# Feed-forward stage: row scaling moved to ScalarE, two small operations per scale, twelve steps written out in a new order

## The chip, the cores and the metric

One NeuronCore of a Trainium2 chip runs the whole program. The metric is the device time of one execution in microseconds. The core has TensorE (PE), VectorE (DVE), ScalarE (ACT), GpSimd (POOL) and a sync queue (SP) that here only starts transfers. Each engine runs its own queue in order, and waits on semaphores that instructions of other engines raise.

## The reference

The reference applies four attention layers and four feed-forward layers to x (8 batches, 256 rows, 256 columns). Only the last feed-forward is touched; x is normalised over its columns first, and the hidden width is 1024:

```python
def act_quant(x):
    scale = 127.0 / jnp.clip(jnp.max(jnp.abs(x), axis=-1, keepdims=True), 1e-05)
    return jnp.clip(jnp.round(x * scale), -128, 127) / scale
...
h = bit_linear(x, w1)
h = depthwise_conv1d(h.transpose(0, 2, 1), conv_w, conv_b)
h = h.transpose(0, 2, 1)
h = jax.nn.silu(h)
return bit_linear(h, w2)
```

`bit_linear` multiplies rows rounded by `act_quant` with weights rounded to -1, 0 and 1. The convolution has three taps along the 256 rows of a batch. The result is added to x. Each row is thus scaled and rounded twice: once before the first product (256 columns), once before the second (1024 columns).

## The kernel before, in words

`build` runs one stage after another. The last is `bit_ffn` (from line 2520); it begins at 1536 us of the span and lasts to the end. A batch has TB = 2 tiles of 128 rows, and the hidden columns are FT = 8 groups of 128 (index f). What happens to a batch, by engine and line:

- VectorE: `norm` (L2615) writes xn for each tile. `token_scale` finds the largest absolute value of each row (amax, L2622) and from it, in four small operations, the factor qs = 127 / max (L2630) and its inverse qr (L2632).
- ScalarE: `rounded` (L2727) writes q1 = xn * qs + MAGIC for each tile; adding MAGIC rounds to a whole number. VectorE: `unrounded` (L2641) writes q2 = (q1 - MAGIC) * qr for each tile.
- TensorE: `turn_tokens` (L2805) transposes q2 into PSUM. ScalarE's `high_part` (L2734) and VectorE's `low_part` (L2646) take it out as xh and xl.
- TensorE: `hidden` (L2817) multiplies for each f, with four matmuls, into one of three PSUM banks. ScalarE's `middle_tap` (L2741), then VectorE's `first_tap` (L2651) and `last_tap` (L2656) apply the convolution. A bank is free when its last tap is done: hidden f waits for the last tap of f - 3, and hidden 0, 1 and 2 for the last taps of f = 6, 7 and 5 of the batch before (lines 2813 to 2815).
- ScalarE: `silu` (L2749) in two halves of four f each. The first silu is preceded by a load of the function table.
- TensorE: `turn_silu` (L2828) transposes one tile at a time into the one PSUM tile pn, 128x1024. The next tile can come in when s1 of the tile before is written (line 2826).
- VectorE: `tile_scale` in six parts: the largest absolute value of each row of pn (L2665), four small operations (L2670 to L2678, which give sqs and sqr), and s1 = pn * sqs + MAGIC (L2683), 128x1024. GpSimd: `whole` (L2787) writes sq = s1 - MAGIC in bf16.
- TensorE: `turn_back` (L2837) transposes sq; ScalarE's `turned_back` (L2756) takes it out as sqT; `product` (L2846) multiplies with the second weights. VectorE's `residual` (L2690) scales by sqr and adds to x. SP stores a batch when both its residuals are done (L2581).

The work is staged in twelve steps, n = 0 to 11. In step n batch n is `new` (norm, token_scale, rounded), batch n - 1 is `turn` (unrounded, turned, split), batch n - 2 is `hid` (hidden and taps), batch n - 3 is `end` (turn_silu, tile_scale, whole) and batch n - 4 is `last` (products, residuals). Steps 4 to 7 have all five and are called full. The order inside a step is written out by hand on each engine: VectorE's loop runs over places (place 2f is the first tap of f, place 2f + 1 the last tap), ScalarE's and TensorE's over f. `every_step` (L2560) writes ten steps as code: 0 to 3, then 4 and 5 in a hardware loop of two turns, which are steps 4 to 7, then 8 to 11. Waits are counted by `upto` (L2573), in the loop from a register.

## Time and profile before

| | |
|---|---|
| Time, three runs | 1704.36, 1704.78 (median), 1707.48 us |
| The profiled execution's own time | 1701.18 us |
| Its span, first to last instruction | 1699.3 us |
| Granted TensorE clock, mean | 0.937 of full |
| Busy over the whole span | TensorE 86%, VectorE 57%, ScalarE 38%, GpSimd 25% |
| The feed-forward stage | 1536.2 to 1699.3 us |

The profiled execution is one run and lies 3.6 us below the median of the timed ones. In its trace an instruction has a start, counted from the beginning of the span, a duration, an engine, a line, and the tiles written and read. The duration of a pipelined instruction is longer than the time until the next one can start.

### The profile page before, as it was taken

Reading aid. Unit: us, or ns where it says so; the run is one execution under the profiler, and the core shown is the slowest. Engines: PE = TensorE matmul, PEld = TensorE weight load, DVE = VectorE, ACT = ScalarE, POOL = GpSimd, SP = SyncE. Lnnn points to the kernel's source line nnn. Section 1 sums busy time; section 2 is a strip of 40 time slices with the busy share of each in tenths; the row PEclk is TensorE's granted clock in tenths of the full one; section 3 lists DMA queues with packets and bytes.
Section 4 is the critical chain, followed back from the end, with each engine's and each line's share of the span. In section 5 each row is a group of like instructions: output and inputs, shape, how many; then the busy total and the mean of one; then the engine's idle time right before and its main releaser. Section 6 shows DMA issues by size and latency. Waiting matters only on the chain. (4 is left out here: it accounts for less than half of the span.)

```text
span 1699.3 us, 32774 instructions
## 1 busy us (share of the span) xinstructions
PE 1460.4 (86%) x11594; PEld 1279.2 (75%) x11594; DVE 971.9 (57%) x2432; ACT 638.2 (38%) x1413; POOL 423.8 (25%) x655
## 2 busy tenths in 40 slices
PE   4789997499977999999997699999999988875765
PEld 3456664489966788888886599999999976654654
DVE  4666763312224676666665655555555547767896
ACT  1233332112214444445443244444444423234553
POOL 2011101133304444434332111100000036730212
PEclk8899999699998999999999799999999999996788
DMA  7655330684410000010000444045337221100000
GB/s 149 114 94 108 67 50 14 236 279 148 133 41 25 8 8 20 20 29 20 8 1 19 159 171 168 30 175 176 132 110 277 87 75 48 34 7 1 14 12 26
DMA packets 97294, 139.83 MB, mean 82 GB/s; under 512 B 10080, under 2 KB 81248, under 8 KB 97056
## 3 DMA queue, kind: packets, MB, share of 16 engines
q1 hardware_dynamic: 79792, 109.83, 22.2%
q0 software_dynamic: 6368, 18.62, 3.8%
q10 hardware_dynamic: 11024, 9.97, 1.9%
q8 instruction: 63, 1.03, 0.3%
q14 instruction: 47, 0.39, 0.1%
HBM read 111.12 MB, written 14.42 MB: 74 GB/s over the span
## 5 line engine op out<-in xcount | busy, mean ns | idle before, releaser
L1867 PE MATMUL f_ph<-f_xgT,f_w 128*128 128x128 f32 x2496 | 285.3, 275 | 2.9 <-issue 2.0
L1867 PEld LDWEIGHTS f_ph<-f_xgT,f_w 128*128 128x128 f32 x2496 | 282.1, 192 | 3.6 <-issue 3.6
L1031 ACT ACTIVATE a_work<-a_ps,a_bias 128x128 f32<-128x128 f32 (+1 forms) x256 | 104.1, 419 | 172.6 <-issue 98.0
L1962 DVE TENSOR_TENSOR f_w_low<-f_w,f_w_high 128x2048 fp32r<-128x2048 f32 x39 | 89.4, 2292 | 99.9 <-ACT f_w_high L1921 99.9
L1231 POOL TENSOR_TENSOR a_work<-a_work,a_recip 128x256 f32<-128x256 f32 (+1 forms) x128 | 103.1, 827 | 147.0 <-DVE a_recip L1150 145.9
L1836 POOL DMA_INDIRECT f_xg<-normed_x,order x39 | 37.1, 952 | 345.2 <-PE f_px L1856 331.6
L574 DVE CUSTOM_DVE_ANT_0 a_shut_s<-a_ps,a_neg 128x256 f32<-128x256 f32 x256 | 93.0, 420 | 39.9 <-PE a_ps L253 39.3
L486 ACT ACTIVATE a_pT<-a_ps 128x1024 f32<-128x1024 f32 x64 | 65.5, 1024 | 119.5 <-PE a_ps L253 119.5
L1921 ACT ACTIVATE f_w_high<-f_w 128x2048 fp32r<-128x2048 f32 x39 | 74.5, 1910 | 85.6 <-DVE f_yg L1974 83.3
L1155 DVE TENSOR_TENSOR a_qk<-a_ps,a_qk 128x512 fp32r<-128x512 f32 x64 | 44.2, 691 | 96.4 <-ACT a_qk L1048 96.4
L1666 PEld LDWEIGHTS f_ph<-f_xgT,f_w 128*128 128x128 f32 x736 | 86.8, 195 | 6.2 <-DMA f_w<-in_f_w 3.0
L1878 PE MATMUL f_py<-f_w_high,f_h_high 128*128 128x256 f32 x312 | 91.4, 293 | 0.0
L1666 PE MATMUL f_ph<-f_xgT,f_w 128*128 128x128 f32 x736 | 87.7, 278 | 3.5 <-DMA f_w<-in_f_w 2.8
L1878 PE MATMUL f_py<-f_w_high,f_h_low 128*128 128x256 f32 x312 | 88.1, 282 | 0.0
L1878 PE MATMUL f_py<-f_w_low,f_h_high 128*128 128x256 f32 x312 | 88.0, 282 | 0.0
L1967 DVE TENSOR_TENSOR f_h_low<-f_raw,f_h_high 128x512 fp32r<-128x512 f32 x78 | 56.4, 723 | 54.3 <-ACT f_h_high L1925 54.3
L1925 ACT ACTIVATE f_h_high<-f_raw 128x512 fp32r<-128x512 f32 x78 | 49.2, 631 | 91.7 <-DVE f_raw L1982 91.7
L1676 PE MATMUL f_py<-f_w,f_hT 128*128 128x256 f32 x368 | 83.5, 380 | 0.2 <-ACT f_hT L1708 0.2
L1747 DVE TENSOR_SCALAR f_hT<-f_ph,f_b 128x128 f32<-128x128 f32 x92 | 25.9, 344 | 88.0 <-PE f_ph L1666 88.0
L1676 PEld LDWEIGHTS f_py<-f_w,f_hT 128*128 128x128 f32 x368 | 68.1, 190 | 9.0 <-issue 0.4
L1708 ACT ACTIVATE f_hT<-f_ph,f_b 128x128 f32<-128x128 f32 x92 | 26.2, 368 | 121.0 <-PE f_ph L1666 121.0
L1132 DVE TENSOR_REDUCE a_top_s<-a_ps 128x2 f32<-128x256 f32 (+1 forms) x128 | 64.1, 542 | 6.2 <-PE a_ps L917 6.2
(348 smaller groups left out, 3465.2 us busy)
## 6 DMA issues: line engine op xcount, KB each, us to landing
f_w<-in_f_w SPq DMA_DIRECT2D x70, 1024.0 KB, 6.8
sorted_y<-f_yg ACTq DMA_DIRECT2D x62, 128.0 KB, 1.7
a_qs<-a_part SPq DMA_DIRECT2D x48, 128.0 KB, 4.3
a_ks<-a_part SPq DMA_DIRECT2D x42, 128.0 KB, 6.2
normed_x<-a_xn SPq DMA_DIRECT2D x16, 256.0 KB, 2.2
x<-in_x SPq DMA_DIRECT2D x8, 256.0 KB, 6.7
a_mask<-in_mask SPq DMA_DIRECT2D x8, 256.0 KB, 6.4
a_maskT<-in_maskT SPq DMA_DIRECT2D x8, 256.0 KB, 6.5
```

Of the source, the lines that this page charges most:

```text
L486: act.activation(pT[:, u // 2 % 2, 2 * (u % 2):2 * (u % 2) + 2, :, :].rearrange("p j t n -> p j (t n)"), ps[:, ST:ST + 2, :], ACT.Exp, sca ...
L574: a = dve.tensor_tensor_reduce(out=shut_s[:, j, t, :], in0=ps[:, bank(m) + j, t * S:(t + 1) * S], in1=neg[:, m // U % 3, t, :], scale=1.0, ...
L1031: act.activation(prob[:, s, i, t * P:(P if t == 0 else TRI)], ps[:, SB + 2 * s + i, t * S:(t * S + P * (t + 1))], ACT.Exp, bias=bias[:, s, ...
L1132: dve.tensor_reduce(top_s[:, s, t, :], ps[:, SB + 2 * s:SB + 2 * s + 2, t * S:t * S + P * (t + 1)], AX.X, ALU.max).then_inc(max_done, 1)
L1231: pool.tensor_tensor(part, part, recip[:, s, t, :].unsqueeze(2).to_broadcast([P, 2, P * (t + 1)]), ALU.mult).then_inc(shares_done, 1)
L1666: mm = pe.matmul(ph[:, q, n, f * P:(f + 1) * P], w[:, s, k, (q * FQ + f) * P:(q * FQ + f + 1) * P], xgT[:, s, k, :], start=(k == 0), stop= ...
L1676: mm = pe.matmul(py[:, s, 0:D], hT[:, s, f, :], w2[:, s, f, :], start=(f == 0), stop=(f == FT - 1))
L1867: mm = pe.matmul(ph[:, q, n, f * P:(f + 1) * P], w[:, s, k, (q * FQ + f) * P:(q * FQ + f + 1) * P], xgT[:, s, k, :], start=(k == 0), stop= ...
L1878: mm = pe.matmul(py[:, s, 0:D], hT[a][:, s, f, :], w2_parts[b][:, s, f, :], start=(f == 0 and n == 0), stop=(f == FT - 1 and n == len(PASS ...
L1921: act.activation(w2_parts[0][:, s, :, :], w2[:, s, :, :], ACT.Copy).then_inc(w2_high, 1)
L1962: dve.tensor_tensor(w2_parts[1][:, s, :, :], w2[:, s, :, :], w2_parts[0][:, s, :, :], ALU.subtract).then_inc(w2_low, 1)
L1967: dve.tensor_tensor(hT[1][:, s, q * FQ:(q + 1) * FQ, :].rearrange("p f n -> p (f n)"), raw[:, q, :], hT[0][:, s, q * FQ:(q + 1) * FQ, :].r ...
```

## The change

The diff is cut to its core. Calls of `upto(pair, ...)` become plain numbers, `every_step` goes, and all twelve steps are written out on each engine by `for n in range(B + 4): step(n)`.

- A scale takes two small operations where it took four: unit = max(maximum, 1e-5) / 127, and its reciprocal. For rows of x, qr is that unit. For hidden rows, sqr = sunit * unit is a small product on GpSimd, in front of `whole`, with a semaphore of its own.
- s1 is written by ScalarE (`scaled`) instead of VectorE.
- The pieces of a step have other places on VectorE, ScalarE, GpSimd and TensorE. For tile 1 `turn_silu`, the reciprocal, s1 and `whole` move into the step after, with batch n - 4; so do silu half 1 (with n - 3) and `turn_back` of tile 0.
- Waits are changed to suit.

```diff
-            def token_scale(pair, b, k):
+            def token_scale(b, k):
 
                 if k == 0:
-                    dve.wait_ge(xn_done, upto(pair, 2 * b + 1, 2))
+                    dve.wait_ge(xn_done, 2 * b + 2)
                     ins = dve.tensor_reduce(amax[:, :], xn[:, :, :], AX.X, ALU.max, apply_absolute_value=True)
                 else:
-                    dve.wait_ge(prep, upto(pair, 5 * b + k - 1, 5))
+                    dve.wait_ge(prep, 3 * b + k)
                 if k == 1:
-                    ins = dve.tensor_scalar(amaxc[:, :], amax[:, :], 1e-5, None, ALU.max)
+                    ins = dve.tensor_scalar(qr[:, :], amax[:, :], 1e-5, 1.0 / 127.0, ALU.max, ALU.mult)
                 if k == 2:
-                    ins = dve.reciprocal(rec[:, :], amaxc[:, :])
-                if k == 3:
-                    ins = dve.tensor_scalar(qs[:, :], rec[:, :], 127.0, None, ALU.mult)
-                if k == 4:
-                    ins = dve.tensor_scalar(qr[:, :], amaxc[:, :], 1.0 / 127.0, None, ALU.mult)
+                    ins = dve.reciprocal(qs[:, :], qr[:, :])
                 ins.then_inc(prep, 1)
...
-                dve.wait_ge(red_done, upto(pair, 5 * i + k - 1, 5 * TB))
+                dve.wait_ge(red_done, 3 * i + k)
                 if k == 1:
-                    dve.tensor_scalar(saxc[:, c], sax[:, c], 1e-5, None, ALU.max).then_inc(red_done, 1)
+                    if i >= TB:
+                        dve.wait_ge(sqr_done, i - TB + 1)
+                    dve.tensor_scalar(sunit[:, c], sax[:, c], 1e-5, 1.0 / 127.0, ALU.max, ALU.mult).then_inc(red_done, 1)
                 if k == 2:
-                    dve.reciprocal(srec[:, c], saxc[:, c]).then_inc(red_done, 1)
-                if k == 3:
-                    dve.tensor_scalar(sqs[:, c], srec[:, c], 127.0, None, ALU.mult).then_inc(red_done, 1)
-                if k == 4:
                     if i >= TB:
-                        dve.wait_ge(resid_done, upto(pair, i - TB, TB))
-                    dve.tensor_scalar(sqr[:, c], saxc[:, c], 1.0 / 127.0, unit[:, 1:2], ALU.mult, ALU.mult
-                                      ).then_inc(red_done, 1)
-                if k == 5:
-                    if i >= TB:
-                        dve.wait_ge(sq_done, upto(pair, i - TB, TB))
-                    dve.tensor_scalar(s1[:, t, :], pn[:, :], sqs[:, c], MAGIC, ALU.mult, ALU.add).then_inc(s1_done, 1)
-
-            def residual(pair, b, t):
-                xs = x[:, pair * (2 * TB) + (b * TB + t), :]
-                dve.wait_ge(o_ready, upto(pair, TB * b + t, TB))
-                if t == 0:
-                    dve.wait_ge(red_done, upto(pair, 5 * (TB * b + 1) + 4, 5 * TB))
+                        dve.wait_ge(s1_done, i - TB + 1)
+                    dve.reciprocal(sqs[:, c], sunit[:, c]).then_inc(red_done, 1)
...
-                for place in range(2 * FT + 2):
-                    if turn and place < TB:
-                        unrounded(pair, n - 1, place)
-                    if end and 3 <= place < 9:
-                        tile_scale(pair, n - 3, 0, place - 3)
-                    if hid and place < 2 * FT:
-                        (first_tap, last_tap)[place % 2](pair, n - 2, place // 2)
-                    if end and place >= 12:
-                        tile_scale(pair, n - 3, 1, place - 12)
-                    if last and place in (3, 8):
-                        residual(pair, n - 4, (3, 8).index(place))
-                    if new and place in (5, 6):
-                        norm(pair, n, place - 5)
+                for place in range(2 * FT):
+                    if last and place == 0:
+                        tile_scale(n - 4, 1, 2)
+                    if turn and place < 2:
+                        unrounded(n - 1, place)
+                    if new and place in (2, 3):
+                        norm(n, place - 2)
+                    if new and place in (4, 8, 10):
+                        token_scale(n, (4, 8, 10).index(place))
+                    if last and place in (5, 12):
+                        residual(n - 4, (5, 12).index(place))
+                    if end and 6 <= place < 9:
+                        tile_scale(n - 3, 0, place - 6)
                     if turn and place == 7:
-                        low_part(pair, n - 1)
-                    if new and place in (9, 10, 12, 14, 16):
-                        token_scale(pair, n, (9, 10, 12, 14, 16).index(place))
-
-            every_step(dve, step)
+                        low_part(n - 1)
+                    if end and place >= 14:
+                        tile_scale(n - 3, 1, place - 14)
+                    if hid:
+                        (first_tap, last_tap)[place % 2](n - 2, place // 2)
...
+            def scaled(b, t):
                 i = TB * b + t
-                act.wait_ge(q_turned, upto(pair, i, TB))
+                act.wait_ge(red_done, 3 * i + 3)
                 if i >= TB:
-                    act.wait_ge(o_ready, upto(pair, i - TB, TB))
+                    act.wait_ge(sq_done, i - TB + 1)
+                act.activation(s1[:, t, :], pn[:, :], ACT.Identity, bias=magic[:, 0:1], scale=sqs[:, t:t + 1]
+                               ).then_inc(s1_done, 1)
...
                 for f in range(FT):
-                    if last and f == 3:
-                        turned_back(pair, n - 4, 1)
                     if hid:
-                        middle_tap(pair, n - 2, f)
+                        middle_tap(n - 2, f)
+                    if last and f == 0:
+                        turned_back(n - 4, 0)
+                    if last and f == 1:
+                        scaled(n - 4, 1)
+                    if end and f == 1:
+                        silu(n - 3, 1)
                     if turn and f == 3:
-                        high_part(pair, n - 1)
-                    if hid and f % 4 == 3:
-                        silu(pair, n - 2, f // 4)
-                    if end and f == 7:
-                        turned_back(pair, n - 3, 0)
-                if new:
-                    rounded(pair, n)
-
-            every_step(act, step)
+                        high_part(n - 1)
+                    if last and f == 4:
+                        turned_back(n - 4, 1)
+                    if end and f == 5:
+                        scaled(n - 3, 0)
+                    if new and f == 6:
+                        rounded(n)
+                    if hid and f == 7:
+                        silu(n - 2, 0)
...
-                pool.wait_ge(s1_done, upto(pair, i, TB))
+                pool.wait_ge(red_done, 3 * i + 2)
                 if i >= TB:
-                    pool.wait_ge(q_turned, upto(pair, i - TB, TB))
+                    pool.wait_ge(resid_done, i - TB + 1)
+                pool.tensor_tensor(sqr[:, t:t + 1], sunit[:, t:t + 1], unit[:, 1:2], ALU.mult).then_inc(sqr_done, 1)
+                pool.wait_ge(s1_done, i + 1)
+                if i >= TB:
+                    pool.wait_ge(q_turned, i - TB + 1)
...
+            def step(n):
+                if is_batch(n - 4):
+                    whole(n - 4, 1)
+                if is_batch(n - 3):
+                    whole(n - 3, 0)
...
-                    if end and f in (2, 6):
-                        turn_silu(pair, n - 3, (2, 6).index(f))
+                    if last and f == 1:
+                        turn_silu(n - 4, 1)
                     if last and f == 2:
-                        product(pair, n - 4, 0)
-                    if turn and f == 3:
-                        turn_tokens(pair, n - 1)
-                    if last and f == 3:
-                        turn_back(pair, n - 4, 1)
+                        turn_back(n - 4, 0)
+                    if turn and f == 4:
+                        turn_tokens(n - 1)
                     if last and f == 4:
-                        product(pair, n - 4, 1)
+                        product(n - 4, 0)
+                    if end and f == 5:
+                        turn_silu(n - 3, 0)
+                    if last and f == 6:
+                        turn_back(n - 4, 1)
                     if hid:
-                        hidden(pair, n - 2, f)
-                if end:
-                    turn_back(pair, n - 3, 0)
-
-            every_step(pe, step)
+                        hidden(n - 2, f)
+                if last:
+                    product(n - 4, 1)
```

## Rows read from the trace of the kernel before

**Rows 1.** Busy time in two steps: length, busy (count) by engine, clock, DMA

```profile
1561.10:1578.80 17.70, 13.37 (x65) 12.02 (x64) 14.86 (x39) 8.81 (x15) 2.93 (x2) 0.60 0.00 0
...
1613.40:1630.50 17.10, 11.56 (x85) 9.79 (x84) 16.07 (x41) 9.35 (x16) 3.67 (x3) 0.90 0.05 15
```

**Rows 2.** Waits of VectorE, 1613.4 to 1647.6: us in total, times, longest

```profile
DVE f_q L2641 <- ACT f_q L2727: 2.9, 3, 1.1
```

**Rows 3.** Timeline of VectorE, start and duration: first taps, a last tap, a residual

```profile
1548.45 0.48 DVE L2651 SCALAR_TENSOR_TENSOR f_y<-f_ph,t_cwu,f_y 128x256 f32<-128x256 f32 x1 [0.59 <-ACT f_y L2741]
...
1562.07 0.48 DVE L2651 SCALAR_TENSOR_TENSOR f_y<-f_ph,t_cwu,f_y 128x256 f32<-128x256 f32 x1 [0.59 <-ACT f_y L2741]
...
1579.72 0.47 DVE L2651 SCALAR_TENSOR_TENSOR f_y<-f_ph,t_cwu,f_y 128x256 f32<-128x256 f32 x1
...
1648.78 0.47 DVE L2651 SCALAR_TENSOR_TENSOR f_y<-f_ph,t_cwu,f_y 128x256 f32<-128x256 f32 x1
...
1663.92 0.48 DVE L2651 SCALAR_TENSOR_TENSOR f_y<-f_ph,t_cwu,f_y 128x256 f32<-128x256 f32 x1 [0.86 <-ACT f_y L2741]
...
1675.32 0.48 DVE L2656 SCALAR_TENSOR_TENSOR f_y<-f_ph,t_cwu,f_y 128x256 f32<-128x256 f32 x1
...
1694.38 0.48 DVE L2690 SCALAR_TENSOR_TENSOR x<-f_po,f_sqr,x 128x256 f32<-128x256 f32 x1 [4.77 <-PE f_po L2846]
```

**Rows 4.** Timeline of GpSimd and VectorE at the end of a full step

```profile
1629.69 1.89 POOL L2787 TENSOR_TENSOR f_sq<-f_s,f_magic 128x1024 bf16<-128x1024 f32 x1 [5.40 <-DVE f_s L2683]
...
1630.47 1.25 DVE L2641 TENSOR_SCALAR f_q<-f_q,f_qr 128x256 f32<-128x256 f32 x1 [0.95 <-ACT f_q L2727]
...
1632.05 0.33 DVE L2641 TENSOR_SCALAR f_q<-f_q,f_qr 128x256 f32<-128x256 f32 x1
```

**Rows 5.** Timeline of VectorE in a full step

```profile
1620.96 1.27 DVE L2683 TENSOR_SCALAR f_s<-f_pn,f_sqs 128x1024 f32<-128x1024 f32 x1
1622.15 0.47 DVE L2651 SCALAR_TENSOR_TENSOR f_y<-f_ph,t_cwu,f_y 128x256 f32<-128x256 f32 x1
...
1623.33 0.67 DVE L2622 TENSOR_REDUCE f_amax<-f_xn 128x2 f32<-128x512 f32 x1
...
1625.22 1.21 DVE L2665 TENSOR_REDUCE f_sax<-f_pn 128x1 f32<-128x1024 f32 x1
1626.35 0.16 DVE L2628 RECIPROCAL f_rec<-f_amaxc 128x2 f32<-128x2 f32 x1
```

**Rows 6.** Timeline of ScalarE, and a row of the page's part 5

```profile
1552.34 1.28 ACT L2749 ACT_TABLE_LOAD   x1
...
1627.89 1.06 ACT L2749 ACTIVATE f_sT<-f_y 128x1024 f32<-128x1024 f32 x1 [2.95 <-DVE f_y L2656]
1628.86 1.00 ACT L2756 ACTIVATE f_sqT<-f_pb 128x1024 bf16<-128x1024 bf16 x1
1629.76 1.08 ACT L2727 ACTIVATE f_q<-f_xn,f_magic,f_qs 128x256 f32<-128x256 f32 x2
...
L486 ACT ACTIVATE a_pT<-a_ps 128x1024 f32<-128x1024 f32 x64 | 65.5, 1024 | 119.5 <-PE a_ps L253 119.5
```

**Rows 7.** Timeline of TensorE: three at the low clock, four at the full

```profile
1569.55 1.97 PE L2828 MATMUL f_pn<-ident,f_sT 128*128 128x128 f32 x8 [2.65 <-DVE f_s L2683]
1571.17 0.78 PE L2817 MATMUL f_ph<-f_xh,t_w1q 128*128 128x258 f32 x2
...
1573.04 1.08 PE L2837 MATMUL f_pb<-identb,f_sq 128*128 128x128 bf16 x8
...
1639.50 1.09 PE L2828 MATMUL f_pn<-ident,f_sT 128*128 128x128 f32 x8 [1.74 <-DVE f_s L2683]
1640.35 0.48 PE L2817 MATMUL f_ph<-f_xh,t_w1q 128*128 128x258 f32 x2
...
1641.48 0.62 PE L2837 MATMUL f_pb<-identb,f_sq 128*128 128x128 bf16 x8
...
1652.96 1.05 PE L2846 MATMUL f_po<-t_w2q,f_sqT 128*128 128x256 bf16 x8 [0.57 <-ACT f_sqT L2756]
```

More of the change, by code:

```diff
@@ L2609, in _, with norm @@
             step(dve.tensor_tensor(rstd[:, :], guess[:, :], total[:, :], ALU.mult))
-            def norm(pair, b, t):
-                row = pair * (2 * TB) + (b * TB + t)
+            def norm(b, t):
+                row = b * TB + t
                 if b >= 1:
-                    dve.wait_ge(q1_done, upto(pair, 2 * b - 1, 2))
-                dve.tensor_scalar(xn[:, t, :], x[:, row, :], mean[:, bass.ds(row, 1)], rstd[:, bass.ds(row, 1)],
+                    dve.wait_ge(q1_done, 2 * b)
+                dve.tensor_scalar(xn[:, t, :], x[:, row, :], mean[:, row:row + 1], rstd[:, row:row + 1],
@@ L2690, in residual @@
+                    dve.reciprocal(sqs[:, c], sunit[:, c]).then_inc(red_done, 1)
+            def residual(b, t):
+                xs = x[:, b * TB + t, :]
+                dve.wait_ge(o_ready, TB * b + t + 1)
+                dve.wait_ge(sqr_done, TB * b + t + 1)
                 dve.scalar_tensor_tensor(out=xs, in0=po[:, 0:D], scalar=sqr[:, t:t + 1], in1=xs,
                                          op0=ALU.mult, op1=ALU.add).then_inc(resid_done, 1)
-            def step(pair, n):
+            def step(n):
@@ L2716, in _ @@
+            for n in range(B + 4):
+                step(n)
         @block.scalar
@@ L2737, in middle_tap, with silu @@
                 i = FT * b + f
-                act.wait_ge(h_ready, upto(pair, i, FT))
+                act.wait_ge(h_ready, i + 1)
                 if b >= 1:
-                    act.wait_ge(silu_done, upto(pair, 2 * (b - 1) + f // 4, 2))
+                    act.wait_ge(silu_done, 2 * (b - 1) + f // 4 + 1)
                 act.activation(y[:, f, :], ph[:, f % BANKS, 1:S + 1], ACT.Identity, bias=cb[:, f:f + 1],
                                scale=cwu[:, f, 1:2]).then_inc(y0_done, 1)
-            def silu(pair, b, half):
+            def silu(b, half):
@@ L2776, in _ @@
+                    if end and f == 5:
[4 more added lines that the diff above has]
+                        silu(n - 2, 0)
+            for n in range(B + 4):
+                step(n)
         @block.gpsimd
@@ L2806, in turn_tokens, with hidden @@
                 mm.then_inc(x_turned, 1)
-            def hidden(pair, b, f):
+            def hidden(b, f):
                 if f == 0:
-                    pe.wait_ge(x_low, upto(pair, b))
+                    pe.wait_ge(x_low, b + 1)
                     if b == 0:
@@ L2814, in hidden @@
                 if FT * b + before >= 0:
-                    pe.wait_ge(y2_done, upto(pair, FT * b + before, FT))
+                    pe.wait_ge(y2_done, FT * b + before + 1)
                 for i, (part, k) in enumerate((part, k) for part in (xh, xl) for k in range(DK)):
```

112 lines of the change are left out of this document (52 added, 60 removed).

## Prediction, made before the changed kernel was run

> **What bounds the stage now.** I read first the busy time by step [rows 1]: in a full step of the feed-forward (17.1 us) VectorE is busy 16.07 us, TensorE 11.56, ScalarE 9.35, GpSimd 3.67. The reader is to see one engine that is nearly full and three that are not. Next the waits of VectorE [rows 2]: in two full steps it waited 2.9 us over three visits, always at the first q2 for ScalarE's q1. Then the times at which VectorE starts the first tap of a batch [rows 3]: batch 0 at 1548.45, batch 1 at 1562.07, batch 2 at 1579.72, batch 6 at 1648.78, batch 7 at 1663.92. So the steps for batches 0 and 1 take 13.6 and 17.65 us, the next five 84.2 together. After batch 7's first tap there are 11.4 us to its last tap (1675.32) and 19.54 more to the end of the last residual (1694.86) [rows 3]. The stage is these six numbers; outside it nothing changes.
>
> A last row shows a loss that the busy time hides. GpSimd's subtraction runs from 1629.69 for 1.89 us; VectorE's q2, started at 1630.47, takes 1.25 us and ends 0.14 after it, while its twin takes 0.33 [rows 4]. Five steps show it, 0.7 to 0.9 each. The Trainium skill (SBUF — State Buffer, on the port pair shared by VectorE and GpSimd) says such operations exclude each other for a whole instruction; the trace agrees.
>
> **What VectorE sheds.** An instruction costs it the time to the next start [rows 5]: s1 1.19 us, a 1024-wide maximum 1.13; elsewhere the duration less 0.08: amax 0.59, a tap or residual 0.39, q2 0.25 and norm 0.32 (durations of 0.47, 0.33 and 0.40); the low part 0.60 and a small operation about 0.08 (estimates from neighbouring starts). Two s1 go (2.4), six small operations (0.5), the wait and lock at q2 (1.7): about 4.6 of 17.2, so VectorE's own work in a full step is 12.6: 16 taps 6.3, and 0.1 more for each of four second taps that directly follow the first (their result is needed), maxima 2.26, amax 0.59, residuals 0.78, norms 0.64, q2 0.5, low part 0.60, six small ones 0.5.
>
> **What comes in its place.** Two 1024-wide operations go to ScalarE. Its rows of that width are 1.02 us from PSUM, 1.06 for silu, 0.90 to 0.97 to the next start [rows 6]; I take 0.97. As bounds: not below 0.90, not above VectorE's 1.27. ScalarE's load becomes some 11 us of 17 and is no bound by itself. The Trainium skill (Trainium Architecture — The Big Picture, table of the engines) says ScalarE is not for simple arithmetic, VectorE being up to about 3 times faster per element. By that s1 would be nearly 3.8 us and the sum some 5 us per step worse. The rows at equal width speak against it. The tiny GpSimd product (nearest small operation, 0.15 on VectorE; bounds 0.1 and 0.3) lies before its wait for s1 and costs nothing; were s1 not awaited, it would delay sq by its length.
>
> **Which waits appear.** Count from the start of the last tap of a step (0). TensorE at full clock [rows 7]: hidden 0.5 us (0.77 to its result), eight f32 transposes 0.85 (1.09), bf16 transposes 0.42 (0.62), product 0.80 (1.05). A handover is 0.05.
> - A. ScalarE takes sqT of tile 0 ahead of its middle tap 1. That sqT needs TensorE's turn_back at f=2, behind hidden 1, which needs the last tap: 0.47 + 0.05 + 0.5 + 0.62 = 1.64; sqT to 2.6; middle tap (0.56, the width of q1, of which two take 1.08 [rows 6]) to 3.2. VectorE's work before the tap ends at 2.1: idle 1.1.
> - B. ScalarE then does s1 of tile 1 and silu half 1 (1.94) ahead of middle tap 2: tap at 5.6, VectorE ready at 4.9: idle 0.7.
> - C. The residual of tile 1 (place 12) needs the product, behind hidden 7, which needs the last tap of f=4: 0.47 + 0.05 + 0.5 + 1.05 + 0.04 = 2.1 after that tap's start; VectorE has 1.4 of work: idle 0.7.
> - D. The maximum of tile 1 (place 14) needs turn_silu, which stands behind the next batch's hidden 0, and that waits for the last tap of f=6 directly ahead of it: 0.52 + 0.5 + 1.09 + 0.04 = 2.15 against 0.39: idle 1.75.
> Sum at full clock: 12.6 + 1.1 + 0.7 + 0.7 + 1.75 = 16.9 us per full step, against 17.1. Thus nearly all that VectorE sheds returns as waits. Step 8, without norm and amax, keeps these waits: 16.8, where now 15.14 of the 84.2 are spent (the norm, amax and q1 wait fall away there today).
>
> At the lower clock (1.2 GHz) a hidden is 0.9, the f32 transposes 1.65 (1.97), the product twice 0.8 [rows 7]. A grows by 0.8, the maximum of tile 0 now waits 1.6 for turn_silu, C grows to 1.9, D to 3.4: 21.6 us. Granted clock is 0.90 in a full step now [rows 1], thus a fifth at the lower level. After a wait of 2.65 us for VectorE the transposes at 1569.55 run at the lower level, after one of 1.74 those at 1639.50 at the full one [rows 7]. I take the same fifth: 16.9 + 0.2 x 4.7 = 17.8. Bounds: none and all.
>
> **Sum.**
> - Head. The maximum of batch 1 moves ahead of batch 0's low part and two small operations of each scale go (0.2 each time), so ScalarE has q1 of batch 1 done and turns to middle tap 0 earlier: first tap of batch 0 at 1547.45, 1.0 us earlier. In the next step the table load (1.28 [rows 6]) and silu half 0 (1.06) now sit between middle taps 3 and 4, and silu half 1 ahead of q1, on which the next first tap waits. After the change all three lie behind middle tap 7. Walked at 1.2 GHz, as the clock is there: TensorE's hidden 3 to 7 pace the taps, the last tap of f=7 starts 9.05 after the first tap; ScalarE, free 0.65 before that, has table load, silu (0.97) and middle tap 0 (0.56) to do, 2.8 in all: next first tap 11.25 after the last one instead of 13.6. The step for batch 1 has VectorE's 12.6 less two residuals and a small operation, 11.7, plus 1.6 for the maximum of tile 0 and 3.0 for D at this clock, plus 0.3 in shorter waits; A, B and C aren't there yet: 16.6 instead of 17.65. Together 1.0 + 2.4 + 1.0 = 4.4 earlier; bounds -7 and -1.
> - Five steps: 4 x 17.8 + 17.7 = 88.9 against 84.2: +4.7; bounds +0.1 (full clock) and +24 (always low).
> - Tail. The step of batch 7 keeps A, B and C: 13.9 from first to last tap instead of 11.4. After it s1 on ScalarE stands behind sqT of the other tile (+0.8) but fewer small steps and an already turned tile save: about 18.5 for 19.54. Together +1.5; bounds -1 and +3.
> - Loops written out: twelve steps for ten. Register operations of 0.1 us vanish; I count 0, bounds -1 and +1. At the turn of the loop the q1 to q2 delay is 0.1 longer than elsewhere, and VectorE is waiting there anyway. The Trainium skill (Runtime: NRT & Kernel Launch, instruction fetch mechanics) says a taken branch can stall the fetch; that would be a gain; these rows show no such stall. The stores run from the sync queue as before, and the last one's cost stays.
> - Total -4.4 + 4.7 + 1.5 = +1.8 us. The profiled execution took 1701.18, so 1703.0 for it. It lies 3.6 below the median 1704.78, and on that scale the forecast is 1706.6. A measurement here can tell about 0.2% (3.4 us) from no change: forecast, no change, with a lean to slower. Its own range is -2 to +6.
>
> **The rivals.**
> 1. VectorE sets the pace. If ScalarE's and TensorE's queues run further ahead than I walked, so that A and B vanish, a step is 15.1 plus 0.9 for the clock: 5 x 16.0 - 84.2 = -4.2, with head and tail -7.1: about 1698. If C and D went as well, 5 x 12.6 gives -21 and a total near -24: 1681. For it: VectorE is today's bound [rows 1]. Against it: C and D follow from the order of TensorE's queue and cannot be hidden by any lead. 18%.
> 2. TensorE keeps its full clock, the forecast otherwise: +0.1 for the five steps, -2.8 in all: 1702. Against it: waits D and A leave TensorE idle for 1.6 and 2.5 us at a stretch. 14%.
> 3. Slower: the low clock lasts. In D hidden and turn_silu come after an idle stretch and run on VectorE's path. From half the time at the lower clock a step is 19.2, +7 for the five over the forecast, total +9: 1714; at all of it 1726. For it: today the granted clock in the step of batch 1 is 0.60 [rows 1], with a fuller TensorE. Against it: from hidden 1 to turn_silu, work at the lower clock stands nearly without a gap, after which rows show the clock high. 23%.
> 4. The change doesn't do what it says: s1 on ScalarE could wait behind its queue so long that VectorE's maximum waits for PSUM. In the walk s1 of tile 0 ends at 10.7 and turn_silu is due at 14: no sign. Included in 3.
> Forecast: 45%.
>
> **Chances.** Faster by over 0.2%: rival 1 (0.18) and 0.10 of rival 2, whose time lies at the edge: 0.28. Slower: rival 3 (0.23) and 0.13 of the forecast, whose range passes the edge: 0.36. Within: the other 0.32 of the forecast and 0.04 of rival 2, 0.36. The range 1694 to 1718 takes in half of rival 1 and rival 3 up to two thirds of the time at the lower clock.
>
> **What would show it.** In the changed profile VectorE should be busy about 13 of 17 to 18 us in a full step, and wait in four places: first tap for middle tap (A, B, about 1.8 a step), residual for product (0.7), and above all maximum for turn_silu (1.75 or more). The f32 rounding should be ScalarE rows of 1.0 us; q2 should be 0.34 throughout. First tap of batch 2 should come 3 to 6 us earlier and first taps of later batches lie 17 to 18.5 apart. Wrong if the maximum waits under 1 us a step, or if steps are under 16 us or over 19.

## The result, and the profile after

Seventeen runs of each kernel on one chip: 1710.34 us after (1703.94 to 1719.52) against 1704.36 before (1698.65 to 1711.12). The ratio of the times, after over before, is 1.0039, 95% interval 1.0024 to 1.0053, so the change costs 4 to 9 us. All ratios below are to the kernel before, the 95% interval in brackets. The profiled execution of the changed kernel took 1705.11 us (span 1703.0, mean granted clock 0.938), 3.9 us more than the one before.

The stage was cut at the same marks as in the prediction: from VectorE's first instruction of the stage to the end of the last residual. All in us.

| | before | after | after, second profile | forecast |
|---|---|---|---|---|
| start to first tap of batch 0 | 12.20 | 11.11 | 11.11 | 11.2 |
| step batch 0 to 1 | 13.62 | 11.34 | 11.35 | 11.25 |
| step batch 1 to 2 | 17.65 | 16.27 | 16.65 | 16.6 |
| four full steps, together | 69.06 | 69.16 | 73.46 | 71.2 |
| step batch 6 to 7 | 15.14 | 18.74 | 18.73 | 17.7 |
| batch 7, first to last tap | 11.4 | 15.19 | 15.19 | 13.9 |
| last tap to end | 19.54 | 18.15 | 18.16 | 18.5 |
| stage | 158.61 | 159.96 | 164.65 | 160.4 |

The stage starts at 1538.66 us after and 1536.25 before, and in the profiles of the experiments anywhere from 1531.7 to 1545.9, though nothing ahead of it differs. So the stage is read from its trace, and the total from the timed runs.

The busy time of five steps of the kernel after (length, busy and count by engine, granted clock, DMA), the last of them the step without a new batch:

```profile
1577.40:1594.60 17.20, 10.52 (x85) 8.63 (x85) 12.73 (x33) 11.42 (x17) 4.17 (x4) 1.00 0.05 17
1594.60:1611.80 17.20, 10.55 (x85) 8.65 (x86) 12.73 (x33) 11.42 (x17) 4.16 (x4) 1.00 0.05 16
1611.80:1629.20 17.40, 11.76 (x85) 9.93 (x86) 12.91 (x34) 11.45 (x17) 4.16 (x4) 0.90 0.05 16
1629.20:1646.50 17.30, 11.65 (x85) 9.92 (x85) 12.80 (x33) 11.45 (x17) 4.17 (x4) 0.90 0.05 17
1646.50:1665.30 18.80, 13.28 (x84) 11.18 (x84) 11.32 (x28) 10.50 (x15) 4.17 (x4) 0.70 0.05 15
```

In [rows 1] VectorE was busy 16.07 of 17.1 us. Now it is busy 12.8 of 17.3 and no engine is full, yet the step is as long as before. The waits of VectorE in the stage say why (us in total, times, longest):

```profile
DVE f_sax L2645 <- PE f_pn L2824: 17.7, 9, 3.1
DVE f_y L2631 <- ACT f_y L2716: 16.9, 14, 2.7
DVE x L2662 <- PE f_po L2842: 14.3, 10, 5.4
DVE f_q L2621 <- ACT f_q L2702: 1.4, 2, 0.7
```

The wait of [rows 2] (q2 for q1) is gone from the full steps (its two visits lie ahead of the first tap of batch 0); three others have come. One full step in VectorE's timeline has them at four places:

```profile
1609.46 1.23 DVE L2645 TENSOR_REDUCE f_sax<-f_pn 128x1 f32<-128x1024 f32 x1 [1.78 <-PE f_pn L2824]
...
1611.59 0.34 DVE L2621 TENSOR_SCALAR f_q<-f_q,f_qr 128x256 f32<-128x256 f32 x1
...
1614.41 0.48 DVE L2631 SCALAR_TENSOR_TENSOR f_y<-f_ph,t_cwu,f_y 128x256 f32<-128x256 f32 x1 [1.12 <-ACT f_y L2716]
...
1616.91 0.48 DVE L2631 SCALAR_TENSOR_TENSOR f_y<-f_ph,t_cwu,f_y 128x256 f32<-128x256 f32 x1 [0.70 <-ACT f_y L2716]
...
1623.64 0.48 DVE L2662 SCALAR_TENSOR_TENSOR x<-f_po,f_sqr,x 128x256 f32<-128x256 f32 x1 [0.76 <-PE f_po L2842]
...
1626.81 1.23 DVE L2645 TENSOR_REDUCE f_sax<-f_pn 128x1 f32<-128x1024 f32 x1 [1.78 <-PE f_pn L2824]
```

From one maximum to the next it is 17.35 us: 1.12 (A), 0.70 (B), 0.76 (C) and 1.78 (D) are waits, 4.36 in all, with the prediction's letters. None of VectorE's waits in the stage ends on GpSimd, so its small product delays nothing there. The q2 takes 0.34, where the lock of [rows 4] made it 1.25. ScalarE in that step:

```profile
1612.90 1.02 ACT L2739 ACTIVATE f_sqT<-f_pb 128x1024 bf16<-128x1024 bf16 x1 [3.74 <-PE f_pb L2833]
1613.82 0.56 ACT L2716 ACTIVATE f_y<-f_ph,t_fb,t_cwu 128x256 f32<-128x256 f32 x1
1614.27 1.20 ACT L2731 ACTIVATE f_s<-f_pn,f_magic,f_sqs 128x1024 f32<-128x1024 f32 x1
1615.36 1.06 ACT L2724 ACTIVATE f_sT<-f_y 128x1024 f32<-128x1024 f32 x1
```

It idles 3.74 us at sqT for TensorE's transposes and only then comes to the middle tap that VectorE awaits. The rounding f_s takes 1.20 us, 1.09 to the next start.

### The profile page after: what moved, and what is told of

It is laid out like the page before. It is cut to its first block and busy times, and to the rows that moved or that the text cites. A ratio compares the mean times of both kernels' runs of the same rounds, so it can differ in the third digit from the quotient of the medians.

```text
span 1703.0 us, 32484 instructions
## 1 busy us (share of the span) xinstructions
PE 1464.5 (86%) x11594; PEld 1279.8 (75%) x11594; DVE 946.0 (56%) x2368; ACT 655.4 (38%) x1429; POOL 426.6 (25%) x671
## 3 DMA queue, kind: packets, MB, share of 16 engines
q8 instruction: 64, 1.05, 0.3%
## 5 line engine op out<-in xcount | busy, mean ns | idle before, releaser
L486 ACT ACTIVATE a_pT<-a_ps 128x1024 f32<-128x1024 f32 x64 | 65.5, 1024 | 119.2 <-PE a_ps L253 119.2
L2813 PE MATMUL f_ph<-f_xh,t_w1q 128*128 128x258 f32 x128 | 36.6, 374 | 42.2 <-DVE f_y L2636 40.5
```

Source lines behind the costliest of these rows:

```text
L486: act.activation(pT[:, u // 2 % 2, 2 * (u % 2):2 * (u % 2) + 2, :, :].rearrange("p j t n -> p j (t n)"), ps[:, ST:ST + 2, :], ACT.Exp, sca ...
L2813: mm = pe.matmul(ph[:, f % BANKS, 0:S + 2], w1q[:, k, f * P:(f + 1) * P], part[:, b % 2, k, :], start=(i == 0), stop=(i == 2 * DK - 1))
```

## The experiments

The theory: each of the four waits comes from the place of one piece in TensorE's or ScalarE's queue, and they hide what VectorE has shed. The first four runs move one piece each, then all three. In the step function of TensorE (and ScalarE in the last) f counts the hidden products; "full step" means batch 2 to 3 and on.

**D alone.**

```diff
-                    if last and f == 1:
+                    if last and f == 0:
                         turn_silu(n - 4, 1)
```

> The changed kernel with one piece moved on TensorE: turn_silu of tile 1 stands ahead of the next batch's hidden 0, not behind it. Order theory: wait D (1.78 us of VectorE for the transposes of tile 1) exists only because of that place. It vanishes in the six steps that have it, a full step falls from 17.35 to about 15.6 us, the time falls by 10.5 us, ratio to the kernel before about 0.998 where the changed kernel has 1.004. Rival, the lower clock: what is lost is lost to TensorE's clock; then the granted clock stays about 0.90 in a full step and the gain is under 4 us, ratio over 1.0015. Rival, ScalarE as bound (11.45 us busy of 17.35 a step): the wait moves to middle taps and a step stays over 16.8.

Measured: 1695.97 us against 1702.91, ratio 0.9959 (0.9933 to 0.9985). The waits of VectorE:

```profile
DVE f_y L2631 <- ACT f_y L2716: 16.9, 14, 2.0
DVE x L2662 <- PE f_po L2842: 15.4, 10, 4.7
DVE f_sax L2645 <- PE f_pn L2824: 6.3, 4, 2.4
```

D is gone from the full steps (the waits for turn_silu, 17.7 us in nine visits, became 6.3 in four), A, B and C stayed at 1.13, 0.71 and 0.76 at the full clock, and three of the four full steps were 15.4 us where they had been 17.2 to 17.4. The fourth took 17.4 at a granted clock of 0.81, with A at 2.02 and C at 1.91. This one move beats the kernel before; the theory held.

**A alone.**

```diff
-                    if last and f == 2:
+                    if last and f == 1:
                         turn_back(n - 4, 0)
```

> The changed kernel with turn_back of tile 0 one place earlier on TensorE, ahead of hidden 1. Order theory: waits A (1.13 us) and B (0.70) of VectorE for the middle taps 1 and 2 come from ScalarE standing in sqT of tile 0. A vanishes, B shrinks to about 0.6: 1.2 us less per step in five to six steps, 6 us in all, ratio about 1.000. Rival, the lower clock: under 2 us. Rival, ScalarE as bound: A's wait reappears in full at tap 2, so A and B still sum to 1.8 and nothing is gained.

Measured: 1705.70 us, ratio 1.0015 (0.9993 to 1.0037). A went and B fell to 0.55, as the theory has it, but the total moved by only 1 to 4 us against the changed kernel's two comparisons (1.0021 and 1.0039), where 6 were expected. A late step, waits at the right:

```profile
1635.15 0.48 DVE L2631 SCALAR_TENSOR_TENSOR f_y<-f_ph,t_cwu,f_y 128x256 f32<-128x256 f32 x1 [0.55 <-ACT f_y L2716]
1636.25 0.48 DVE L2662 SCALAR_TENSOR_TENSOR x<-f_po,f_sqr,x 128x256 f32<-128x256 f32 x1 [0.62 <-PE f_po L2842]
1637.61 1.22 DVE L2645 TENSOR_REDUCE f_sax<-f_pn 128x1 f32<-128x1024 f32 x1 [0.48 <-PE f_pn L2824]
1643.05 0.48 DVE L2662 SCALAR_TENSOR_TENSOR x<-f_po,f_sqr,x 128x256 f32<-128x256 f32 x1 [0.76 <-PE f_po L2842]
1646.22 1.23 DVE L2645 TENSOR_REDUCE f_sax<-f_pn 128x1 f32<-128x1024 f32 x1 [1.78 <-PE f_pn L2824]
```

The two waits in the middle (residual and maximum of tile 0, 0.62 and 0.48) are new and take back 1.1 us of what A and B gave: a wait removed ahead of others that stay lets VectorE arrive early at the next.

**C alone.**

```diff
+                    if last and f == 7:
+                        product(n - 4, 1)
                     if hid:
                         hidden(n - 2, f)
-                if last:
-                    product(n - 4, 1)
```

> The changed kernel with the product of tile 1 ahead of hidden 7 and not behind it. Order theory: wait C (0.76 us of VectorE for that product) vanishes, 0.75 us a step in six steps, 4 us in all, ratio about 1.0015. Rival: hidden 7 is late instead, and VectorE waits as long for middle tap 7: ratio stays 1.004.

Measured: 1699.54 us, ratio 0.9976 (0.9954 to 0.9999). The residual's waits fell from 14.3 us in ten visits to 11.9 in six. C is gone from two of the four full steps, and the shorter of these took 16.5 us. In the two others, 17.5 us each, it is longer than before:

```profile
1613.24 0.48 DVE L2662 SCALAR_TENSOR_TENSOR x<-f_po,f_sqr,x 128x256 f32<-128x256 f32 x1 [1.04 <-PE f_po L2842]
```

There the product ran at the lower clock (1.93 us, against 1.05 in the step of 16.5), though all three steps have a granted clock of 0.90. So the place is part of C's cause and the clock another. The time fell by 8 to 11 us, more than the 4 expected, and the profile doesn't put the rest down to C: the four full steps together took 69.25 us (69.16 in the changed kernel's first profile), while the step without a new batch and batch 7's taps were at the full clock and took 16.00 and 13.53 us, where they had been 18.74 and 15.19.

**All three.** The three edits together.

> All three moves of TensorE's pieces together. Order theory: the gains add, since each wait has its own cause: 10.5 + 6 + 4 = 20 us, a full step of 13.7 to 14.2 us, ratio about 0.992, faster than both kernels. Rival, ScalarE as bound: with 11.5 us of work and its own waits in line a step stays over 15 us and the gain is under 12 us. Rival, the lower clock: the step varies between 14 and 18 us from batch to batch with the granted clock, and the sum is under 12 us.

Measured: 1680.41 us (1675.18 to 1687.95), ratio 0.9856 (0.9825 to 0.9888), faster than both kernels. The single moves' gains, each against the changed kernel, add up to 0.0167 (counted from its 1.0039) or 0.0113 (from 1.0021), which gives 0.9872 or 0.9908. The first lies within the interval, the second 0.002 outside it, so the total time doesn't show that the moves are worth more together than one by one. Busy time of three steps:

```profile
1581.70:1596.30 14.60, 11.49 (x85) 9.91 (x86) 12.69 (x33) 11.53 (x17) 4.17 (x4) 0.88 0.05 19
1596.30:1609.50 13.20, 10.08 (x85) 8.76 (x86) 12.54 (x34) 11.28 (x17) 4.17 (x4) 1.00 0.06 21
1609.50:1622.60 13.10, 9.98 (x85) 8.67 (x85) 12.44 (x33) 11.39 (x18) 4.17 (x4) 1.00 0.07 22
```

At the full clock the step is 13.14 us with VectorE busy 12.5. The three waits and what B gave up leave 17.2 - 1.12 - 0.76 - 1.78 - 0.15 = 13.4, so within a step the waits add up. One by one, the moves shortened a step by 1.85 (D), 0.15 (A and B) and 0.85 us (C), 2.85 in all, where together they gave 4.1: what the single runs lack is what the waits that stayed took back, as in the run for A. The two full steps of 14.6 have a granted clock of 0.88, and C is back in them with 0.94 and 0.86, the product again at the lower clock (1.93 us). The theory's step (13.7 to 14.2) and ratio (0.992) were short of what came.

**The changed kernel again,** to see how far its stage varies.

> The changed kernel unchanged, for a second profile. The first profile has 160.0 us in the feed-forward stage (158.6 before), 1.4 more, where the medians differ by 6.7. If the stage itself varies with TensorE's clock, this profile's stage is over 162 us and its full steps differ in length by 1 to 2 us; if the difference lies in the stages before it, this stage is again within 1 us of 160 and its start is 2 us or more later than 1536.3.

Measured: 1707.84 us against 1703.18, ratio 1.0021 (1.0001 to 1.0041). The stage took 164.65 us in its profile, 4.7 more than the first time, with the same instructions:

```profile
1577.70:1596.30 18.60, 12.68 (x85) 11.05 (x86) 12.85 (x33) 11.46 (x17) 4.17 (x4) 0.84 0.05 15
1596.30:1613.60 17.30, 11.65 (x85) 9.90 (x86) 12.82 (x33) 11.46 (x17) 4.17 (x4) 0.90 0.05 16
1613.60:1632.70 19.10, 13.44 (x85) 11.31 (x85) 12.75 (x33) 11.45 (x17) 4.17 (x4) 0.70 0.04 14
```

VectorE's and ScalarE's busy times are as before; TensorE's and the clock differ. The four waits hang on TensorE, so they stretch: in the 19.1 us step C is 1.27 and D 3.09, which is the 1.8 us that it is longer than the step of 17.3 ahead of it. TensorE around that D, with waits of 1.58 and 2.23 for VectorE:

```profile
1609.65 0.48 PE L2813 MATMUL f_ph<-f_xh,t_w1q 128*128 128x258 f32 x2 [1.58 <-DVE f_y L2636]
...
1610.21 1.04 PE L2824 MATMUL f_pn<-ident,f_sT 128*128 128x128 f32 x8
1613.47 0.51 PE L2813 MATMUL f_ph<-f_xh,t_w1q 128*128 128x258 f32 x2 [2.23 <-DVE f_y L2636]
...
1627.48 0.77 PE L2813 MATMUL f_ph<-f_xh,t_w1q 128*128 128x258 f32 x2 [1.58 <-DVE f_y L2636]
...
1628.48 1.91 PE L2824 MATMUL f_pn<-ident,f_sT 128*128 128x128 f32 x8
1632.61 0.80 PE L2813 MATMUL f_ph<-f_xh,t_w1q 128*128 128x258 f32 x2 [2.23 <-DVE f_y L2636]
```

Same waits, same work: the transposes took 1.04 us (2.4 GHz) in one step and 1.91 (1.2 GHz) in the next. The Trainium skill (TensorE: Matmul & The Clock Gate, Part 1) says that how many matmuls run slow at a kernel's start varies from run to run of one kernel. The clock in the middle of this stage, of which that sentence doesn't speak, varies between runs too: the same four full steps had 1.00, 1.00, 0.90 and 0.90 in the first profile and 0.84, 0.90, 0.70 and 0.85 in this one.

**Rows scaled by VectorE, the new order otherwise.**

```diff
-                act.activation(s1[:, t, :], pn[:, :], ACT.Identity, bias=magic[:, 0:1], scale=sqs[:, t:t + 1]
+                dve.tensor_scalar(s1[:, t, :], pn[:, :], sqs[:, t:t + 1], MAGIC, ALU.mult, ALU.add).then_inc(s1_done, 1)
```

(issued by VectorE at places 1 and 9 of its step)

> The changed kernel with s1 given back to VectorE: at place 1 for tile 1 (last) and at place 9 for tile 0 (end), order otherwise as changed. VectorE's work rises by 2.4 us a step; A and B vanish, since s1 fills A and ScalarE is free for B; C (0.8) and D (1.8) stay: 17.5 us a step. GpSimd's subtraction of tile 1 then falls on norm of tile 1: by the port lock seen before that costs up to 1 us more, 18.5. Ratio 1.005 without and 1.008 with the lock. Rival, the gain of the change is all in the offload to ScalarE: then a step is 17.35 + 2.4 = 19.7 and the ratio 1.011.

Measured: 1721.69 us (1717.62 to 1727.53), ratio 1.0110 (1.0084 to 1.0135). The four full steps took 20.4 to 23.2 us at granted clocks of 0.60 to 0.84. A and B are gone from them, as the theory has it, D stayed (1.78 and 3.09), and C grew to about 2 in three of them. VectorE's busy time in a step rose by 3.6 us and not 2.4, as the norm of tile 0 took 1.81 us in place of 0.40 beside GpSimd's f_sq in each. So the theory's waits came and its price (17.5 to 18.5 us) was far too low; the total is the one that the rival gave, though not for its reason, since A and B did go. Under this order the offload is worth 0.7 to 0.9%.

**The kernel before without its loops,** all twelve steps written out.

> The kernel before with its twelve steps written out on the four compute engines and nothing else changed. My theory: the loop costs nothing that shows, ratio 1.000 within 0.002, full steps of 17.0 to 17.4 us. Rival, the taken branch stalls the fetch: two loop turns less, over 1 us gained in the first step of each turn. Rival, the longer program moves the whole kernel's time: ratio 1.002 or more with an unchanged stage.

Measured: 1704.30 us, ratio 1.0007 (0.9988 to 1.0025). The loops cost nothing that shows. In its profile the stage took 160.4 us (158.6 in the kernel before): batch 7's taps and the tail were at a lower clock (0.86 and 0.69) and took 13.02 and 21.00 us. So the stage varies in the old order too.

**TensorE kept busy:** six more products of 128x256 (results not used) ahead of hidden 0 and of hidden 1.

```diff
+                if f < 2 and b >= 1:
+                    for _ in range(6):
+                        pe.matmul(px[:, 0, :], w1q[:, 0, 0:P], w1q[:, 0, 0:S], start=True, stop=True)
```

> The changed kernel with six more matmuls (128x256, result not used, into the PSUM tile px while it is free) before hidden 0 and before hidden 1 of every batch but the first, where TensorE idles 1.6 and 2.2 us. Clock theory: granted clock 1.00 in all full steps from early on, a full step of 16.9 us and not 17.35, 3 to 6 us less in all, ratio 1.001 to 1.002. Rival, the clock isn't what costs: steps stay at 17.2 to 17.4 or grow by the added matmuls, ratio 1.004 or more.

Measured: 1704.06 us, ratio 0.9997 (0.9979 to 1.0014). Three steps of it by busy time, the last one without a new batch:

```profile
1592.40:1610.90 18.50, 13.63 (x97) 11.42 (x98) 12.77 (x33) 11.43 (x17) 4.17 (x4) 0.91 0.05 15
...
1628.10:1645.30 17.20, 12.07 (x97) 10.27 (x97) 12.77 (x34) 11.42 (x17) 4.18 (x4) 1.00 0.05 17
1645.30:1662.10 16.80, 11.82 (x96) 9.99 (x95) 11.18 (x27) 10.49 (x15) 4.17 (x4) 1.00 0.05 16
```

The two last ones are at the full clock, and they take what the prediction's walk at full clock gives within 0.3 us: 17.2 for a full step (forecast 16.9) and 16.8 for the last (forecast 16.8), which at a clock of 0.70 took 18.8 in the changed kernel. The two full steps ahead of them still fell to 0.91 and took 18.0 and 18.5 us, though TensorE was busy for some 1.9 us more than in a step of the changed kernel at 0.90. So it is not shown that more work keeps the clock, though the total came out 4 to 7 us under the changed kernel's, about what the theory had (3 to 6). What is shown is what the low clock costs: next to nothing (17.35 against 17.22 us) or 2 us a step, by where it falls on the waits A, C and D.

**The mended order with the rows on VectorE:** the three moves and the edit of the run with the rows scaled by VectorE.

> The kernel with all three pieces moved, and the scaled rows back on VectorE (two of 1.27 us in each full step in place of ScalarE's 1.20). It asks whether handing the rows to ScalarE is worth something only once the order lets it. VectorE's own work in a full step was 12.50 of 13.16 us, so it becomes about 15.0, and every instruction that shares its port with GpSimd's f_sq may be locked. Theory (in the order as changed the waits hide VectorE's work, in the mended order they don't): steps of 15.0 to 16.5 us against 13.14, so 2 to 3 us a step longer, 12 to 20 us in all: ratio to the kernel before 0.993 to 0.999, against 0.9856 with the rows on ScalarE. Rival (the gain of the three moves is one of the order alone, wherever the rows are scaled): steps of 13.2 to 13.8 us and a ratio of 0.985 to 0.989.

Measured: 1697.21 us against 1703.77, ratio 0.9959 (0.9939 to 0.9979). Its full steps take 16.2 us, and VectorE is busy in nearly all of that:

```profile
1599.20:1615.40 16.20, 10.57 (x85) 8.73 (x85) 16.13 (x36) 9.53 (x15) 4.17 (x4) 1.00 0.05 17
```

Against 13.14 that is 3.1 us a step. The two scaled rows are 2 x 1.19 = 2.4, and the wait B of 0.55 is gone; the other 1.2 us are here, in the timelines of GpSimd and VectorE:

```profile
1617.38 1.89 POOL L2780 TENSOR_TENSOR f_sq<-f_s,f_magic 128x1024 bf16<-128x1024 f32 x1 [2.44 <-DVE f_s L2663]
...
1617.61 1.81 DVE L2600 TENSOR_SCALAR f_xn<-x,f_mean,f_rstd 128x256 f32<-128x256 f32 x1
...
1619.74 0.40 DVE L2600 TENSOR_SCALAR f_xn<-x,f_mean,f_rstd 128x256 f32<-128x256 f32 x1
```

The norm starts 0.23 us after f_sq and ends 0.15 after it: 1.81 us in place of 0.40, 1.4 more, and so in all four full steps. The lock of [rows 4] has moved from q2 to another instruction. The theory held, at the long end of its range for a step because of this. The Trainium skill (SBUF — State Buffer, on the port pair) says that where instructions of VectorE and GpSimd both need the shared ports, the one that comes second is blocked for the whole of the other's instruction; the rows agree.

**The old order, one part at a time.** First the small operations alone, in the kernel before (its token scales; the tile scales likewise):

```diff
-                    ins = dve.tensor_scalar(amaxc[:, :], amax[:, :], 1e-5, None, ALU.max)
+                    ins = dve.tensor_scalar(qr[:, :], amax[:, :], 1e-5, 1.0 / 127.0, ALU.max, ALU.mult)
...
-                    ins = dve.reciprocal(rec[:, :], amaxc[:, :])
+                    ins = dve.reciprocal(qs[:, :], qr[:, :])
```

> The kernel before with one part of the change alone: two small operations per scale on VectorE in place of four or five (maximum times 1/127 in one, then the reciprocal; the residual's factor stays a third small operation on VectorE, after them). Order, loop, and rows scaled on VectorE stay. Two small operations of 0.15 go per batch and one of 0.15 per tile, about 4 x 0.07 us of VectorE's time in a full step, as they overlap their neighbours. Theory (VectorE has some 16.1 of 17.2 us of work in a step of the kernel before, and its two waits of 1.1 to 1.5 us are behind ScalarE): a step 0.2 to 0.5 us shorter, a ratio of 0.9975 to 0.9995. Rival (the waits take up what is saved): ratio of 1.000 within 0.001.

Measured: 1705.51 us, ratio 1.0012 (0.9995 to 1.0029). No gain shows, which is nearer the rival (1.000 within 0.001) than the theory: VectorE's busy time in a full step fell to between 15.5 and 15.8 us, and yet the steps were 17.9 to 18.4, at granted clocks of 0.78 to 0.88 (0.79 to 0.90 before).

Then also the rows scaled by ScalarE, still in the old order:

```diff
+                    if end and f == 4:
+                        scaled(pair, n - 3, 0)
                     if end and f == 7:
                         turned_back(pair, n - 3, 0)
+                        scaled(pair, n - 3, 1)
```

> The kernel before with the small operations merged as in the run beside it, and the rows scaled by ScalarE: tile 0 behind the middle tap 4, tile 1 as the last but two of ScalarE's step, behind the transposed codes of tile 0. So everything of the change but its order. VectorE's work in a step falls from 16.1 to about 13. Theory (the order is what holds the changed kernel at 17.2): here the waits at the step's seam stay instead (the codes f_q, 1.1 to 1.5 us, and the first taps behind ScalarE), and one of the two scaled rows, 1.2 us of ScalarE, stands on the path over the seam: steps of 15.5 to 17 us, a ratio of 0.990 to 1.000, better than the changed kernel's 1.0039 or 1.0021. Rival (the new order is a gain, and without it the offload pays nothing): steps of 17.5 us or more, a ratio of 1.002 or more.

Measured: 1725.02 us (1723.48 to 1727.77), ratio 1.0125 (1.0096 to 1.0155). The theory fell, the rival stands. A full step by busy time, and the wait of VectorE that ends it:

```profile
1604.70:1624.90 20.20, 13.69 (x86) 11.84 (x85) 13.80 (x36) 11.67 (x17) 3.79 (x2) 0.75 0.05 15
```

```profile
1623.57 1.39 DVE L2637 TENSOR_SCALAR f_q<-f_q,f_qr 128x256 f32<-128x256 f32 x1 [3.71 <-ACT f_q L2716]
```

VectorE has shed its rows and waits 3.71 us for q1, not the 0.95 of [rows 4]. ScalarE there:

```profile
1619.78 1.06 ACT L2738 ACTIVATE f_sT<-f_y 128x1024 f32<-128x1024 f32 x1 [2.25 <-DVE f_y L2652]
1620.74 1.00 ACT L2753 ACTIVATE f_sqT<-f_pb 128x1024 bf16<-128x1024 bf16 x1
1621.64 1.20 ACT L2745 ACTIVATE f_s<-f_pn,f_magic,f_sqs 128x1024 f32<-128x1024 f32 x1
1622.73 1.08 ACT L2716 ACTIVATE f_q<-f_xn,f_magic,f_qs 128x256 f32<-128x256 f32 x2
```

The silu waits for VectorE's last tap, and sqT, the scaled row and q1 stand behind it: VectorE waits for a piece behind one that waits for VectorE, here too. At this pair of places the offload loses 1.1% in the old order; no other pair was tried there.

**Wait B in the mended order:**

```diff
-                    if end and f == 1:
+                    if end and f == 2:
                         silu(n - 3, 1)
```

> The kernel with all three pieces moved, and the second half of ScalarE's silu behind its middle tap 2, not 1. In the run with three pieces moved the only wait of VectorE left in a full step was 0.55 us, its first tap 2 for the middle tap behind that silu and a scaled row. Theory (that wait is the last thing that VectorE does not hide): it goes, steps of 12.6 to 12.8 us at the full clock, 3 us in all: ratio 0.984 within 0.002, against 0.9856. Rival (a wait of the same size turns up behind it, at the first tap 3 or at the silu's transposes): steps of 13.1 us and the same ratio as before.

Measured: 1680.04 us, ratio 0.9869 (0.9839 to 0.9900); the steps are 13.1 and 14.6 us, as without the edit. The rival held: in all four full steps B's 0.55 came back at the maximum of tile 0, behind the silu's transposes.

```profile
1588.33 1.23 DVE L2645 TENSOR_REDUCE f_sax<-f_pn 128x1 f32<-128x1024 f32 x1 [0.53 <-PE f_pn L2824]
```

The ratios to the kernel before, side by side:

| order | rows on VectorE | rows on ScalarE |
|---|---|---|
| old | 1 (small operations merged: 1.0012) | 1.0125 |
| new, as changed | 1.0110 | 1.0039 and 1.0021 |
| new, three pieces moved | 0.9959 | 0.9856 |

## Why the prediction was right, and where its terms were off

The forecast was no change with a lean to slower, +1.8 us on the profiled execution. By the ratios the change measured +6.6 us (4 to 9) and, in a second comparison, +3.6 (0.2 to 7). The predicted 1706.6 lies 3.7 below the first median, and 3.4 us was the bound set for "no change": the first comparison lies beyond it, the second at its edge. The mechanism of the four waits was right, the sum too small, and the price of the lower clock was wrong in both directions.

- **What VectorE sheds.** Forecast: its own work 12.6 us in a full step. Measured: 17.20 - 4.36 = 12.84, busy 12.73. Short by 0.24.
- **The four waits.** Forecast 1.1, 0.7, 0.7 and 1.75; measured 1.12, 0.70, 0.76 and 1.78. Moving the piece took D and A away from every full step, each by itself, so they come from the places of the pieces. C went in two steps of four, and where the product ran at the lower clock it stayed. B was only shifted.
- **The step at full clock.** Forecast 16.9, measured 17.2: the 0.24 above and 0.1 in the waits.
- **The scaled row on ScalarE.** Forecast 0.97 to the next start, bounds 0.90 and 1.27; measured 1.09 (duration 1.20). Mis-sized by 0.12, twice a step. The Trainium skill's factor of up to about 3 (Trainium Architecture — The Big Picture, table of the engines) isn't seen here: 1.20 us against VectorE's 1.27 on the same 128x1024 [rows 5].
- **The lock.** Forecast: gone from q2. It is; with the rows on VectorE it came back, on the norm.
- **Head.** Forecast -4.4; measured 1.09 + 2.28 + 1.38 = 4.75 earlier. Right.
- **The lower clock.** Forecast: 0.9 us for a granted clock of 0.90, as a fifth of 4.7. Measured: the two steps at 0.90 of the first profile took 17.35 us, 0.13 over those at 1.00, with the four waits unchanged; in the second profile one at 0.84 took 18.60 and one at 0.70 19.14. In the list of waits at that clock the prediction gives D as 3.4, without taking off VectorE's own 0.39; its total of 21.6 and its term for batch 1 use 3.0, and 3.09 was measured. C was put at 1.9 there and measured 1.25 in these steps, and in others up to 2.1.
- **Five steps.** Forecast 4 x 17.8 + 17.7. The four full steps were 17.3 each in one profile and 18.4 in the other. That 17.8 is their mean is luck: neither profile has it. The last step is the term that was mis-sized: 18.7 in both, since its granted clock was 0.70, not the 0.90 that the prediction carried over from [rows 1]. At the full clock it takes 16.8, as in the run with TensorE kept busy.
- **Tail.** Forecast 13.9 and 18.5; measured 15.19 and 18.15. Of the 1.3 of the first some 0.9 is the low clock again, as it is 14.29 at a granted clock of 1.00 (D moved, and TensorE kept busy); 0.4 is in the walk. In the second profile the waits from batch 6's first tap to batch 7's were 1.50 (A), 1.49 (B), 1.24 (C) and 3.09 (D), and in batch 7's own step A was 2.74 and B 1.50 (1.85 and 1.5 at the full clock).

These terms are 1.0 + 1.3 - 0.35, some 2 us, so the +1.8 becomes +3.8. The two stages measured 1.35 and 6.04 us over the one before, 3.7 in the mean. That agrees with the second comparison and is just under the low end of the first, but it is less firm than it looks: with its steps written out the old order's stage took 160.4 us, and against the mean of those two the mean is 2.8. Whether more than the clock's variation is in the rest of the first median stays open: the profiled run of that set was itself 5.2 us under its median.

- **Loop.** Forecast 0; measured 1.0007, interval 0.9988 to 1.0025. Right.
- **Rival 1** (VectorE sets the pace) didn't come: all four waits are there. That C and D can't be hidden by a lead follows from the order of the queues, as was argued; no run tried a longer lead. Once A, C and D were removed VectorE did set the pace, at 13.1 us a step at the full clock. The mended kernel took 1680 where the rival's price without waits was 1681, which is luck in part: the five steps took 68.2 us and not 63, and the head saved 7.6 and not 4.4.
- **Rival 2** (full clock): true of two full steps of the first profile, 17.2 us against 17.3 and 17.4 at 0.90. In those steps there was next to no gain in it, as the low stretch missed the waits.
- **Rival 3** (the low clock lasts): true of single steps (0.70 to 0.85, 18.4 to 19.1 us), not of all.
- **Rival 4:** the change does what it says.

So the change is 0.2 to 0.4% slower, and the moves show why. Its order puts turn_silu behind hidden 0, turn_back behind hidden 1 and the product behind hidden 7, and each of these hidden products waits for a last tap of VectorE. VectorE then waits for a piece that waits for VectorE.

## What to carry to other kernels

When work is taken off the fullest engine, look next for such loops: engine X waits for a piece that stands in Y's queue behind another piece that waits for X. By the order of the queues, no lead of one engine can hide such a wait, and here moving three pieces by one place took the ratio from 1.0039 to 0.9856, while the whole change without the moves had gained nothing. The offload itself is worth 1.0% in the mended order (0.9959 to 0.9856) and costs 1.1% in the old one (1.0012 to 1.0125). Price each wait from the start of the last instruction that X gives, and try several such moves together as well, since one alone may hand its gain to the next wait, as A's did.

## What the runs showed of the hardware that was not expected

- Identical code with the same queues took 17.3 or 19.1 us in neighbouring steps, with a granted clock of 0.90 and 0.70, and 17.2 at 1.00. With the product moved, neighbouring steps at the same 0.90 took 16.5 and 17.5 us, the longer with the product at the lower clock. The cost depends on what the low stretch falls on, not on its share alone.
- A 1024-wide rounding that reads a scale and a bias per partition took 1.20 us on ScalarE, a silu of the same width 1.06 and a copy to bf16 1.02. Why wasn't tried.
- A VectorE instruction of 0.40 us took 1.81 when it started 0.23 us after one of GpSimd's.
